# A nine-stage attention chain on one core: new order tables for all engines, and the filling products left out

## The reference

```
L0: mha(x, x, causal, 16 heads of 8)  -> +x, layernorm
    mha(x, context)                   -> +x, layernorm
    fc2(relu(fc1 x)) * mask, +x       -> layernorm
L1: cross attention (16 heads), Wo; x + ff(x), ff = W2 silu(W1 x), 512 wide
L2: causal self attention, cross attention, feed forward (relu, 512 wide)
L3: 3 x [ mha(x, x), 4 heads of 32, relu projections, key and query masks
          -> +x, normalize;  x + leaky_relu(x Wff + bff) ]
```

## Time and profile before

| | |
|---|---|
| median of 3 runs | 1085.9 us (1084.74 to 1085.93) |
| span of the profiled execution | 1085.1 us |
| PE busy | 1005.6 us (93%) |
| PE weight loads busy | 725.6 us (67%) |
| DVE busy | 840.9 us (77%) |
| ACT busy | 635.8 us (59%) |
| POOL busy | 320.4 us (30%) |
| filling products | 581 matmul instructions, 113.4 us busy |
| mean granted TensorE clock | 0.986 |
| data moved | 13.6 MB |

### The profile page before, as it was taken

One profiled execution on the slowest core, in us unless ns is written; L12 is line 12 of the kernel. 1 busy time (PEld: TensorE's weight loads), 2 busy tenths in 40 slices (PEclk: granted clock), 3 DMA queues, 4 the chain that ended last, 5 costly groups with the idle time before them and its releaser, 6 DMA issues.

```text
span 1085.1 us, 38818 instructions
## 1 busy us (share of the span) xinstructions
PE 1005.6 (93%) x16923; PEld 725.6 (67%) x16957; DVE 840.9 (77%) x2336; ACT 635.8 (59%) x938; POOL 320.4 (30%) x405
## 2 busy tenths in 40 slices
PE   8889988899999999999999998889999999998996
PEld 5657665576777677767776776556767677677674
DVE  5897999867476756789878899999567774679986
ACT  5346565567777464555645655556777766464652
POOL 4022245511000113346450313553011020336531
PEclk9999999999999999999979999999999999999998
DMA  7000000000000000000010000000000000000001
GB/s 255 3 22 23 2 3 3 2 2 2 3 3 3 12 9 14 11 2 2 2 31 2 3 13 3 2 2 2 3 2 3 3 3 3 1 2 2 2 2 40
DMA packets 13722, 13.60 MB, mean 13 GB/s; under 512 B 617, under 2 KB 13170, under 8 KB 13298
## 3 DMA queue, kind: packets, MB, share of 16 engines
q1 hardware_dynamic: 13554, 11.11, 3.2%
HBM read 9.01 MB, written 2.10 MB: 10 GB/s over the span
## 4 chain that ended last, share of the span: by engine, by line
PE 42%; DVE 28%; ACT 5%; issue 3%; POOL 2%; POOLq 0%; DVEq 0%; ACTq 0%
PE pair L708 8%; DVE mx L1363 7%; PE pair L916 7%; PE pair L911 5%; PE pair L782 4%; PE pair L695 4%; PE pair L935 3%; DVE stats L1085 3%; PE pair L815 2%; DVE Y L1164 2%; ACT PT L1011 2%; PE pair L702 2%; PE pair L683 2%; DVE Y L1108 2%; PE pair L949 2%
## 5 line engine op out<-in xcount | busy, mean ns | idle before, releaser
L1011 ACT ACTIVATE PT<-pair 128x1024 f32<-128x1024 f32 x184 | 180.3, 1029 | 124.8 <-PE pair L916 115.7
L1363 DVE TENSOR_REDUCE mx<-pair 128x16 f32<-128x1024 f32 x184 | 218.4, 1215 | 42.1 <-PE pair L916 41.6
L916 PEld LDWEIGHTS pair<-KQ 32*128 32x128 f32 (+3 forms) x4416 | 170.7, 157 | 37.6 <-DVE mx L1363 3.4
L916 PE MATMUL pair<-KQ 32*128 32x128 f32 (+3 forms) x4416 | 180.0, 254 | 2.4 <-DVE mx L1363 1.0
L708 PE MATMUL pair<-xf,W_all 128*128 128x512 f32 x336 | 177.4, 623 | 3.2 <-ACT xf L977 1.0
L1390 POOL TENSOR_SCALAR ve<-mv 128x4 f32<-128x4 f32 x64 | 17.0, 265 | 503.3 <-DVE mv L1088 432.5
L683 PE MATMUL pair<-warm 128*128 128x512 bf16 (+3 forms) x581 | 113.4, 395 | 17.8 <-DVE Y L1164 7.8
L977 ACT ACTIVATE KQ<-pair,c 128x512 f32<-128x512 f32 x160 | 100.3, 692 | 42.9 <-PE pair L708 42.2
L935 PE MATMUL pair<-PT,V 128*32 128x64 f32 x5120 | 94.2, 221 | 2.2 <-ACT PT L1011 0.7
L977 ACT ACTIVATE V<-pair 64x512 f32<-64x512 f32 x128 | 79.1, 618 | 26.5 <-PE pair L815 24.7
L935 PEld LDWEIGHTS pair<-PT,V 128*32 128x32 f32 x5120 | 78.3, 110 | 22.2 <-issue 8.7
(11 more groups left out here) (122 smaller groups left out, 1824.0 us busy)
## 6 DMA issues: line engine op xcount, KB each, us to landing
W_all<-weights SPq DMA_DIRECT2D x1, 2880.0 KB, 13.7
Xin<-x SPq DMA_DIRECT2D x8, 256.0 KB, 3.6
C<-ctx SPq DMA_DIRECT2D x8, 256.0 KB, 4.1
out<-X SPq DMA_DIRECT2D x8, 256.0 KB, 2.5
row<-rows SPq DMA_DIRECT2D x1, 1024.0 KB, 6.1
c<-const SPq DMA_DIRECT2D x1, 504.0 KB, 5.5
W_all<-weights SPq DMA_DIRECT2D x1, 192.0 KB, 2.9
c<-const SPq DMA_DIRECT2D x1, 80.5 KB, 2.0
```

The lines of the kernel that those rows point to most:

```text
L916: last[u] = pe.matmul(banked[u // 2][:, at:at + 2 * S], stationary[rows_, seq].rearrange("p r t -> p (r t)"), moving[rows_, seq].rearrange ...
L1011: act.activation(PT[:, place, :], banks.of("B", a, s, v)[:], ACT.Exp, scale=float((D // (2 * PAIRS[a])) ** -0.5)).then_inc(*banks.drain((" ...
L1363: dve.tensor_reduce(dst, banks.of("A", a, s, v)[:].rearrange("p (u m t) -> p u m t", u=2, t=S), AX.X, ALU.max).then_inc(*banks.drain(("A", ...
```

## The change

The four texts of `ORDER` are written anew. Every step of before is there once in after: 1152 on PE, 776 on ACT, 849 on DVE, 176 on POOL. The order and the banks differ from the first line on. No PE entry has a `+n`: of the 244 entries that carried one (323 repetitions in all) none is left, so `fill` stays in the code and is never called. A fifth text, `SP`, holds the loads and stores; it lists them in the order in which before issued them. PE remembers the output bank of a stream for each half apart, since `v2` may now stand ahead of `v0` and `v1`; and `A`/`B` halves may be taken with `v0` between them.

```diff
 ORDER = {
     "PE": """
-        0.0.0 x@7+1; 0.0.1 x@6; 0.0.0 pq@7 pk@6; 0.0.3 x@5; 0.0.1 pq@4+1; 0.0.2 x@7; 0.0.1 pk@3 pv@2+1; 0.0.0 pv@6
+        0.0.0 x@0; 0.0.1 x@1; 0.0.0 pq@0 pk@1; 0.0.1 pq@2 pk@0; 0.0.2 x@3; 0.0.0 first@1; 0.0.3 x@2; 0.0.0 length@1;
...
+    "SP": """
+        1.0.0 xin; 1.0.1 xin; 1.0.2 xin; 1.0.3 xin; 1.0.0 cin; 1.0.1 cin; 1.0.2 cin; 1.0.3 cin; 0.8.0 out; 0.8.1 out;
+        0.8.2 out; 0.8.3 out; 1.8.0 out; 1.8.1 out; 1.8.2 out; 1.8.3 out
+    """,
 }
@@
-                for section.group in range(1, GROUPS):
-                    for s in range(STREAMS):
+                def step(name, a, s):
+                    if name == "xin":
                         sp.wait_ge(*vec.at("sum", 1, s, ago=1))
...
-                for section.group in range(GROUPS):
-                    for s in range(STREAMS):
+                    elif name == "out":
...
+                walk("SP", step)
+                section.group = GROUPS - 1
@@
                     if v % 2 == 0:
-                        outputs[s] = room("OT", a, s, v // 2)
+                        outputs[s, v // 2] = room("OT", a, s, v // 2)
```

More of the change, by code:

```diff
@@ L58 @@
[L58 to L72, removed]
@@ new lines @@
+        0.0.2 pq@3; 0.0.0 maskrow@1; 0.0.1 pv@4; 0.0.0 A0@03; 0.0.2 pk@3; 0.0.0 A1@20; 0.0.3 pq@2 pk@3; 0.0.0 pv@4;
+        0.0.1 first@2; 0.0.2 pv@3; 0.0.3 pv@4; 0.0.2 first@5 length@3; 0.0.1 length@2 maskrow@2; 0.0.0 maxrow@0; 0.0.2
+        maskrow@1; 0.0.0 B0@23; 0.0.1 A0@01; 0.0.0 B1@32; 0.0.1 A1@01; 0.0.0 v2@6 v0@7 v1; 0.0.2 A0@12; 0.0.1
+        maxrow@7; 0.0.0 t0@0 v3; 0.0.3 first@1; 0.0.0 t1@4; 0.0.1 B0@31; 0.0.3 length@0; 0.0.2 A1@21; 0.0.1 v0@1 v1
+        B1@31; 0.0.2 maxrow@1; 0.1.0 x1@4; 0.0.1 t0@5; 0.1.0 kv@2; 0.0.1 v2@3 v3; 0.1.0 pq@1 pk@2; 0.0.3 maskrow@0;
@@ new lines @@
+        0.0.2 B0@23; 0.0.1 t1@2; 0.1.0 pv@3; 0.0.2 v0@0; 0.1.0 first@1; 0.0.2 v1; 0.1.0 length@1; 0.0.3 A0@12; 0.0.2
+        t0@0; 0.0.3 A1@31; 0.1.1 x1@1; 0.1.0 maskrow@1; 0.0.2 B1@23; 0.1.1 pq@1; 0.1.0 A0@13; 0.0.2 v2@4; 0.0.3
+        maxrow@5; 0.0.2 v3; 0.1.1 kv@1; 0.1.0 A1@12; 0.1.1 pv@1; 0.0.2 t1@6; 0.1.1 pk@7; 0.0.3 B0@20; 0.1.1 first@6;
+        0.0.3 B1@01 v0@4 v1; 0.1.1 length@5; 0.1.0 maxrow@6; 0.3.0 ctx@7; 0.0.3 v2@0; 0.2.0 kv@1; 0.0.3 v3 t0@6; 0.1.0
+        B0@12; 0.0.3 t1@0; 0.1.1 maskrow@1; 0.1.2 x1@7; 0.1.0 v0@6; 0.1.2 kv@2 pq@3; 0.1.0 v1; 0.1.1 A0@02; 0.1.2
@@ new lines @@
+        pk@2; 0.1.0 t0@6; 0.1.2 pv@7; 0.1.1 A1@01; 0.1.2 first@4; 0.5.0 ksum@5; 0.1.0 B1@03; 0.1.2 length@4; 0.2.0
+        pk@6; 0.1.2 maskrow@4; 0.5.0 pv@7; 0.1.0 v2@0 v3; 0.1.1 maxrow@1; 0.5.1 ksum@4; 0.1.2 A0@13; 0.2.0 pv@0; 0.1.0
+        t1@1; 0.1.1 B0@30; 0.1.3 x1@6 kv@7; 0.1.2 A1@10; 0.1.3 pq@6 pv@7; 0.1.1 B1@13; 0.1.2 maxrow@0; 0.1.1 v0@1 v1
+        v2@2; 0.1.3 pk@3; 0.1.1 t0@1 v3; 0.2.0 x1@3; 0.1.1 t1@2; 0.1.2 B0@03; 0.2.0 fc1@3 fc2@0; 0.1.2 v0@1 B1@13 v1;
+        0.1.3 first@6; 0.1.2 v2@7 v3 t0@0; 0.2.1 kv@1; 0.1.2 t1@2; 0.1.3 length@3; 0.3.1 ctx@6; 0.2.1 pk@7; 0.1.3
@@ new lines @@
+        maskrow@2; 0.8.0 ff@0; 1.0.0 x@1; 0.7.2 A0@1; 0.7.3 x1@4; 1.0.0 pq@1 pk@0; 0.7.3 ff@4; 1.0.0 pv@1; 0.7.2
+        maxrow@0; 1.0.0 first@5; 0.7.2 B0@0; 0.8.1 x1@2; 1.0.0 length@3; 0.7.3 x@4; 0.7.2 v0@5 v1@3; 0.7.3 pk@4; 0.8.1
+        ff@2; 1.0.1 x@3; 1.0.0 maskrow@5; 0.7.3 ksum@0 pq@1 pv@4; 1.0.1 pv@3; 0.7.3 maskrow@2; 1.0.1 pq@0 pk@1; 0.7.3
+        A0@2; 1.0.0 A0@13; 0.8.2 x1@0; 1.0.1 first@1; 0.8.2 ff@0; 0.7.3 maxrow@1; 1.0.2 x@2; 1.0.0 A1@23; 0.7.3 B0@1;
+        1.0.2 pq@0; 1.0.0 maxrow@1; 1.0.1 length@4; 1.0.2 pv@5; 0.7.3 v0@1 v1@2; 1.0.1 maskrow@3; 1.0.2 pk@4; 1.0.0
@@ new lines @@
+        B0@03; 1.0.1 A0@12; 1.0.0 v0@0 v1 B1@23 t0@0; 1.0.2 first@1; 1.0.1 A1@13; 1.0.0 v2@0; 0.8.3 x1@1; 1.0.2
+        length@4; 1.0.0 v3; 0.8.3 ff@1; 1.0.3 x@0; 1.0.1 maxrow@5; 1.0.0 t1@2; 1.0.2 maskrow@3; 1.0.3 pk@0 pq@1; 1.0.1
+        B0@23; 1.0.3 pv@0; 1.0.2 A0@13; 1.0.1 v0@0 v1 B1@23; 1.1.0 x1@0; 1.0.1 t0@1; 1.1.0 kv@2; 1.0.1 v2@3 v3; 1.0.2
+        A1@23; 1.1.0 pq@0 pk@1 pv@2; 1.0.1 t1@0; 1.0.2 maxrow@3; 1.0.3 first@4; 1.1.0 first@5; 1.0.3 length@4; 1.0.2
+        B0@01; 1.1.0 length@5; 1.5.0 ksum@6; 1.1.0 maskrow@7; 1.0.3 maskrow@0; 1.0.2 v0@1 v1 B1@12; 1.1.1 x1@7; 1.0.3
@@ new lines @@
+        pq@0; 1.1.0 t1@1; 1.1.1 v0@2; 1.1.0 t0@3; 1.1.1 B1@32; 1.1.2 length@3; 1.1.1 v1; 1.1.3 kv@0; 1.2.0 pv@1; 1.1.1
+        v2@2; 1.1.2 maskrow@3; 1.1.1 t0@6 v3; 1.2.0 pk@7; 1.1.3 pk@0; 1.1.2 A0@12; 1.1.3 pv@1; 1.1.1 t1@6; 1.1.2
+        A1@10; 1.1.3 first@4; 1.2.1 kv@5; 1.1.3 length@4; 1.3.2 ctx@2; 1.2.2 kv@3; 1.2.1 pk@5; 1.1.2 maxrow@2; 1.2.1
+        pv@0; 1.1.3 maskrow@1; 1.1.2 B0@13; 1.5.1 pv@4 maskrow@5; 1.1.3 A0@01; 1.1.2 v0@6 v1 B1@03; 1.2.0 x1@4; 1.1.3
+        A1@13; 1.2.0 fc1@4; 1.2.2 pk@5; 1.2.0 fc2@4; 1.2.1 x1@0; 1.1.2 v2@1 v3; 1.2.1 fc1@0; 1.1.2 t1@1 t0@5; 1.2.1
```

492 lines of the change are left out of this document (241 added, 251 removed).

## The result

After takes 1089.4 us (median of 20 runs, 1084.6 to 1097.8), before 1086.1 (20 runs, 1082.9 to 1088.7). The ratio is 1.0042, with a 95% interval from 1.0029 to 1.0056: 0.42% slower, 4.6 us, where the prediction had 1075 us and faster. (The medians lie 3.3 us apart and the means 4.4; the ratio is used throughout.) Runs in which the chip was in a slower state are left out of the ratios. The profiled execution of after is among its slower ones (span 1093.2 us, granted clock 0.946; the median clock of its 20 runs is 0.949), so sizes are taken from medians and the trace is read for places.

A forecast was written before the change was run, and what follows sets the result against it. No engine bounds it throughout: PE is full in stages 3 to 6, DVE in stages 0 to 2. -18.1 - 1.9 - 5.5 + 12 + 2.7 = -10.8 gave 1075 us; forecast range 1065 to 1083.7, overall 1054 to 1106.

The forecast's parts named there:

- clock term of long falls: Stage 0 of group 0 and group 1: new narrow-product clusters, one more long fall in all, +2.7 us; bounds -2.7 and +11.
- Filling gone: Stages 3 to 6: removing filling products shortens the chain that ended last, -18.1 us; bounds 0 and 33.9.
- Short falls: Mostly stages 0 to 2: PE without filling has 12 more clock falls at 1.0 us each, +12; bounds 0 and +41.
- Order and moved values: Attention 5 values leave stages 3 to 6, key mask goes to stages 1 and 2: -1.9 us; fewer PE waits: -5.5.
- The sign that these stretches shorten by some 15 us: Stages 3 to 6: shortening by some 15 us in all would show the filling term right.
- The DVE sign: From 120 to 200 us: DVE's busy share staying above 94% would help show the moved values right.
- The long falls' places: Soon after 20 us and in stage 1 of group 1: clock at 0.50 for more than 6 us.
- A: Stages 0 to 2: the clock gives back more than the filling cost; 1095 us, from 1088 to 1115; chance 0.27.
- B: PE isn't full, filling lay in waits that stay: +7, 1093 us, from 1085 to 1098; chance 0.15 beyond no change.
- C: Stages 3 to 6: the whole 33.9 us won, hardly any fall added; 1049 us, from 1048 to 1065; chance 0.12.
- D: Whole kernel: the terms cancel, no change that can be told, 1083.7 to 1088.1 us; chance 0.10.
- the sign on PE's busy time: Whole kernel: PE busy near 890 to 930 us, from 1005.6 - 113.4 = 892 plus time at half speed.

The follow-up runs named there:

- experiment 1: Old filling put back in after's new order: 1128.4 us, ratio 1.0381; all filling taken out of before's old order: 1084.4 us, ratio 0.9985.
- wide `first`: Each product of `first` computes its 8 columns eight times over: on after 1080.5 us, 0.9957; on the old order without filling 1079.3 us, 0.9930.
- the square: Before's old order on one chip, `first` narrow or wide: ratios 1 and 0.9970 with all the filling, 0.9985 and 0.9942 without.

## Why the prediction was wrong

What the clock costs can be read inside a kernel. Over the 20 runs of after, mean clock and time go together with -754 us per unit of clock (correlation -0.88; clock 0.942 with 1094.4 us, 0.956 with 1084.6); over the runs of before it is -607, -666, -537 and -673 in the four batches, over those of experiment 1's old order -616; the extremes among kernels with ten runs or more are -504 (the same old order again) and -886 (before with wide `first`). I take 6.5 us for 0.01. A correlation alone doesn't tell which causes which: a run with a longer wait is late and falls as well. The widening is an intervention that takes no PE time, and it bought 0.013 of clock and 9.2 us in the new order (7.1 for 0.01, across two chips), 0.009 and 4.7 us in the old one (5.2, on one chip). The table of marks agrees too: up to the first mark after with wide `first` takes 229.7 us with 27 low and with narrow 237.6 with 51, the like of 7 us for 0.01. So the price is about right, and it is the only thing that splits the two measured differences below; the split is worked out, not measured.

| part | predicted, us | measured or worked out, us |
|---|---|---|
| filling gone, without the clock | -18.1 | -14.0 |
| short falls that this adds (12, 42 us low) | +12.0 | +12.4 (0.019 of clock, 41 us low) |
| their sum, the old order without filling | -6.1 | -1.6, measured |
| order and moved values, without the clock | -7.4 | -6.8 |
| falls that the order adds (one, 14 us low) | +2.7 | +13.0 (0.020 of clock, 44 us low) |
| their sum, the new order | -4.7 | +6.2, measured |
| all | -10.8 | +4.6, measured |

**The step that failed** is the clock term of long falls, "one more in all, +2.7". I counted clusters of narrow products in the order and nothing else. The new order spends 111 us at the low level instead of the 67 that the old order without filling has (0.949 and 0.969). Of these 44 us about 11 lie with `first`: widening takes 28 us of low time off the new order and 17 off the old (0.013 and 0.008 of clock, the latter the mean of 0.007 and 0.009). Where the rest lies, the two profiled executions show (120.9 us low in after, 67.3 in the old order of experiment 1): 17 us more at 700 to 740, 16 more after 1050, 10 more from 150 to 210, 10 more from 460 to 540, 7 more before 130, and 7 less from 540 to 700. In those at 168 and 711 us, PE has waits ahead of the fall and goes on having them inside it; I read their length so, that PE at half speed makes DVE and through it itself late again, but no run tested this alone. The second trace of the old order without filling (75.7 us low) gives the same three first places: 17, 18 and 14 more. By the price of 6.5 the step is 10 of the 15 us by which the sum was off; by 5 us for 0.01 it would be 7 (and the filling term another 7), by 8.8 it would be all 15. That the order adds 44 us of low level is measured; what they cost is an estimate.

**Filling gone** was mis-sized, 14.0 against 18.1, 4 us of the miss, and it was in the wrong place; that its total comes near is partly luck. I had it in the PE-full stretches (11.9 of the chain's 18.1 us lie in them, 7.9 between the marks) and added nothing for stages 0 to 2. But the widened layers, between those marks, became only 3.2 and 1.3 us shorter in the two traces of the old order without filling, and the filling outside stages 0 to 2 gave 2.4 us for 0.005 of clock, so 5 to 6 without it. The rest of the 14.0, some 8 us, must lie in stages 0 to 2. The bound of 33.9 was too high as well: with the overlap of modelled ends taken off, filling covers 15.2 us in these two stretches that no other product covers. In the same way PE's own work in the DVE-full stretches was 235.4 us, not 207.9, and the lower bound for PE busy 950, not 892.

**Short falls** came out as predicted in time at the low level and in price, less so in number: the two traces of the old order without filling have 12 and 16 low stretches (67 and 76 us) against six (32 us) of before, some of them 6.8 and 10.2 us long.

**Order and moved values** agree as a sum (-7.4 and -6.8). By place they agree in one half: from the old order without filling to after the widened layers become 12.1 us shorter (14.0 by the second trace), where six of the eight moved values, 9 us, had stood and -12.2 - 5.5 was forecast. What happened outside was not separated from the clock, so the near equality of the sums may be luck. The sign that these stretches shorten by some 15 us came true (15.3), but for another reason than the filling it was to show. `pv` with its bias product stands from 119.5 us on, as the sign asked (eight products of L821 between 119.5 and 211.9 us). The DVE sign failed: DVE is busy 86.3 of 100 us from 120 to 220, not over 94%.

```profile
120.00:220.00 100.00, 80.04 (x1704) 61.24 (x1704) 86.34 (x275) 56.45 (x82) 38.02 (x43) 0.88 0.01 2
```

So what made me call this stretch DVE-full held for the old order only: the new one leaves DVE 13.7 us idle there although it has more work. "The prediction is wrong if DVE's idle time in stages 0 to 2 doubles" was the right sign; it grew 1.8 times.

**The long falls' places:** a low stretch soon after 20 us came (35.4 us, 6.8 long), where two `first` and three `pv` stand together. In group 1 the pair of `first` at 595 us gave only 3.4 us, and the 13.7 us at 550 us of before went. The order rows pointed at half of it.

**The rivals.** A had the mechanism: the clock gives back more than the filling cost. Its time came, at the low end (1089.4 in 1088 to 1115, against 1095); its clock, under 0.93, did not (0.949), and half of the clock's loss came from the order (0.020 of 0.039), not from the filling. The Trainium skill ("TensorE: Matmul & The Clock Gate", A second HAM failure mode: psum-queue depth-cycling) describes a PE that idles briefly between groups of matmuls and keeps falling back to the low clock; the long fall at 711 us fits that, with waits of 0.4 to 2.3 us between its groups, though they end with DVE and ACT and no run shows PSUM banks behind them; I had weighed only the rule on activity, not this one. B had the time too (1085 to 1098) with another reason: that the filling lay in waits that stay. In the PE-full stretches this is nearly what the traces show (1.3 to 3.2 us of the 7.9 between the marks). For the whole kernel the square speaks against it with wide `first` (0.28%, intervals [0.9955, 0.9984] and [0.9925, 0.9960] that just touch), and can't tell with narrow ones. C, D and the forecast are out. Both signs that would have shown A or the forecast (clock under 0.93, about 0.96) missed on either side; the sign on PE's busy time (890 to 930 us) was passed by 36 us, since it took all 113.4 us of filling off.

What stays open: which steps of the new order make the holes at 14 us (PE waits 3.1 us for `Qf`), 168 and 711 us, and what the values of attention 5 are worth alone. No run holds the clock up in the new order without taking PE time in the places of the long falls, so their cost rests on the price above.

## What to carry to other kernels

Price an order in two currencies, the waits it removes and the time that TensorE spends at the low clock; here, by the estimate above, a new order won 7 us of the first and paid 13 of the second. In this kernel the filling products were worth about what they cost, and cost much more in an order for which they weren't placed. Don't subtract the busy time of products from that of their engine: where modelled ends overlap, half of it stays. Look first for real products that could carry more columns in the time of their weight load. Compare variants by the clock of each run as well as by its time, and repeat the corner on which a claim rests on one chip.
